# Settling stage of a two-layer kernel: TensorE adds the input, the row factors run one unit behind, rows are stored whole

## What is computed

```python
x = x + attn0(layernorm(x)) + ffn0(layernorm(x))   # ffn0: top 2 of 16 experts by row, plus shared ones
xn = layernorm(x)
x = x + attn1(xn) + ffn1(xn)

def ffn1(input, weight, alpha, bias):              # w_ternary holds only -1, 0 and 1
    return einsum('bsd,od->bso', input, w_ternary * alpha) + bias
# attn1: rows scaled by x / norm(x), times 16 * (gamma + 1), then q, k, v of 16 heads, softmax, output projection
```

## Time and profile before

| | before |
|---|---|
| median of 3 runs | 3088.47 us (3084.22 to 3092.26) |
| the profiled execution, its own time | 3087.61 us |
| its span in the trace | 3085.9 us |
| route and experts, 0 to 598 us | PE busy 494.42 us |
| settle, 598 to 848 us | PE busy 124.87 us, DVE 206.95 us, granted clock 0.62 |
| second layer, from 856 us | PE busy nearly throughout |

### The profile page before, as it was taken

How to read it: one execution, slowest core, us unless ns; L and a number is a source line. 1 busy time by engine, 2 the same in 40 slices (tenths; PEclk the granted TensorE clock), 3 DMA queues, 4 the chain that set the end, 5 groups by cost and what they waited for, 6 DMA issues and landing times.

```text
span 3085.9 us, 46913 instructions
## 1 busy us (share of the span) xinstructions
PE 2810.6 (91%) x13282; PEld 2085.5 (68%) x13282; DVE 2055.1 (67%) x3489; ACT 1839.9 (60%) x2667; POOL 2002.8 (65%) x1246
## 2 busy tenths in 40 slices
PE   6999588655579999999999999999999999999997
PEld 4777456444456777777777777777777777777775
DVE  6887322288866767677676767677676667766763
ACT  4555112122257777777776767777777777777774
POOL 4776400177537777777777777777777777777775
PEclk9999799866689999999999999999999999999998
DMA  4432355588732222222222222231322222232321
GB/s 137 136 123 91 120 172 183 184 257 251 218 87 58 52 73 53 67 60 63 72 48 72 51 69 60 60 78 42 79 46 73 55 64 62 58 77 43 79 47 47
DMA packets 267556, 283.00 MB, mean 92 GB/s; under 512 B 97344, under 2 KB 206144, under 8 KB 267328
## 3 DMA queue, kind: packets, MB, share of 16 engines
q1 hardware_dynamic: 255168, 248.25, 30.0%
q0 software_dynamic: 12288, 33.57, 3.5%
HBM read 131.76 MB, written 82.31 MB: 69 GB/s over the span
## 4 chain that ended last, share of the span: by engine, by line
PE 69%; ACT 1%; DVE 1%; POOL 1%; issue 0%; DMA 0%; SPq 0%; POOLq 0%; ACTq 0%; DVEq 0%
PE psV_b L1527 8%; PE psV_b L1522 7%; PE psV_b L1523 7%; PE psS_b L1510 7%; PE psS_b L1509 7%; PE psN_b L1495 7%; PE psY_b L1450 4%; PE psX_b L1450 4%; PE psY_b L1452 4%; PE psY_b L1451 4%; PE psX_b L1451 4%; PE psX_b L1452 4%; POOL pp_lo_b L1240 1%; PE psN_b L1579 0%; DVE vals_lo_b L1418 0%
## 5 line engine op out<-in xcount | busy, mean ns | idle before, releaser
L1240 POOL TENSOR_TENSOR pp_lo_b<-pf_b,pp_hi_b 128x1024 fp32r<-128x1024 f32 x512 | 1229.8, 2402 | 605.6 <-ACT pp_hi_b L1282 519.8
L1386 DVE TENSOR_REDUCE negmax_b<-psN_b 128x2 fp32r<-128x1024 f32 x512 | 627.1, 1225 | 378.5 <-PE psN_b L1495 370.7
L1277 ACT ACTIVATE pf_b<-psS_b 128x1024 f32<-128x1024 f32 x512 | 526.0, 1027 | 238.9 <-PE psS_b L1510 235.9
L1509 PE MATMUL psS_b<-qA_b,kA_b 128*128 128x512 f32 x1024 | 405.8, 396 | 6.8 <-DVE qB_b L1401 4.9
L1510 PE MATMUL psS_b<-qB_b,kB_b 68*128 68x512 f32 x1024 | 406.6, 397 | 0.0
L1523 PE MATMUL psV_b<-pp_hi_b,vals_lo_b 128*64 128x512 f32 x1024 | 403.5, 394 | 0.0
L1522 PE MATMUL psV_b<-pp_hi_b,vals_hi_b 128*65 128x512 f32 x1024 | 401.8, 392 | 1.4
L1495 PE MATMUL psN_b<-kA_b,qA_b 128*128 128x512 f32 x1024 | 322.5, 396 | 4.6 <-DVE negmax_b L1386 4.1
L1301 ACT ACTIVATE kA_b<-psX_b 64x512 fp32r<-64x512 f32 x256 | 152.0, 594 | 289.7 <-PE psX_b L1452 284.9
L1527 PE MATMUL psV_b<-pp_lo_b,vals_hi_b 128*65 128x512 f32 x1024 | 320.1, 394 | 5.0 <-POOL pp_lo_b L1240 5.0
L1282 ACT ACTIVATE pp_hi_b<-pf_b 128x1024 fp32r<-128x1024 f32 x256 | 271.5, 1061 | 8.1
(11 more groups left out here) (201 smaller groups left out, 5454.4 us busy)
## 6 DMA issues: line engine op xcount, KB each, us to landing
kA_b<-kA_b SPq DMA_DIRECT2D x128, 256.0 KB, 2.9
qB_b<-qA_b SPq DMA_DIRECT2D x128, 256.0 KB, 2.9
inverse_b<-inverse_dram SPq DMA_DIRECT2D x256, 128.0 KB, 3.0
xs_e<-rows_dram SPq DMA_DIRECT2D x144, 128.0 KB, 2.0
results_dram<-ys_e SPq DMA_DIRECT2D x72, 256.0 KB, 2.4
x_a<-x_dram SPq DMA_DIRECT2D x16, 512.0 KB, 4.8
part_dram<-acc_a SPq DMA_DIRECT2D x32, 256.0 KB, 2.1
acc_s<-part_dram SPq DMA_DIRECT2D x32, 256.0 KB
```

Of the source, the lines that this page charges most:

```text
L1240: pool.tensor_tensor(pp[1][:, c], pf[:, c], pp[0][:, c].bitcast(F32), ALU.subtract).then_inc(pl_pool, 1)
L1277: a.activation(pf[:, c], psS[:], ACT.Exp).then_inc(exp_act, 1)
L1386: v.tensor_reduce(negmax[:, n.slot(2), 2 * c:2 * c + 2], psN[:], AX.X, ALU.max, negate=True).then_inc(mx_dve, 1)
L1509: pe.matmul(psS[:, t], kA[:, s, keys], qA[:, s], start=True, stop=False)
```

## The change

Seven edits, the first five in settle:

1. DVE's addition of `x` (L938) goes. PE adds it in `psA`: for each tile an fp32 matmul of `x` with the identity, 256 columns, and then the transposes of `acc` as two ordinary fp32 matmuls that accumulate on it.
2. `xrt` is one fp32 tile, stored whole. DVE's remainder (L921) goes, the ternary weights are fp32, and four fp32 matmuls stand where eight fp32r ones stood.
3. The addition of the last bias (L958) goes from settle; `finish` reads `x1`. In phase_b, DVE adds the bias to `acc` in steps 3 to 6 of the next batch.
4. DVE's loop is `gathered(u)`, `factors(u-1)`, `finish(u-2)`. `f_dve` counts the factors by themselves.
5. `acc` and `x` of the first three units are loaded in the experts' stage (`Ahead`), POOL gathers two units before its loop, and SP loads `gamma` and the first weights behind unit 3.
6. phase_b loads whole rows into two slices of `ot_hi` (`raw_x`) in step 11, and splits them itself: ACT in step 12 (`rows_high`), DVE in steps 12 and 13 (`rows_low`). `otf`'s copies to those slices wait for it.
7. Batch 0 is split at phase_b's start, between the first weights' splits.

```diff
@@ experts, SP @@
+                if n >= PAIRS - 5 and n < PAIRS - 2:
+                    ahead.load(sp, n - PAIRS + 5)
@@ settle, POOL @@
-            for u in range(3):
-                gather(u)
+            gather(0)
+            gather(1)
             for u in range(NU):
-                need(g, s_dve, SD, u, 9)
-                need(g, s_dve, SD, u - 2, SD)
+                need(g, s_dve, SD, u, SD)
+                need(g, f_dve, FC, u - 2, FC)
...
-                gather(u + 3)
+                if u < 2:
+                    gather(u + 2)
+                if u >= 1:
+                    gather(u + 3)
@@ settle, ACT @@
-                need(a, s_dve, SD, u, SD)
+                need(a, f_dve, FC, u, FC)
@@ settle, DVE @@
-                v.tensor_tensor(acc[:, u % 4], psA[:, u % 2].rearrange("p (t d) -> p t d", t=U), x[:, u % 4],
-                                ALU.add).then_inc(s_dve, 1)
...
-                rows_low(u - 1)
-                v.tensor_tensor(x1b[:, u % 3], x1[:, u % 3], fbias_bc[:].unsqueeze(1).to_broadcast([P, U, D]),
-                                ALU.add).then_inc(s_dve, 1)
...
+            for u in range(NU + 2):
+                if u < NU:
+                    gathered(u)
+                if 0 <= u - 1 < NU:
+                    factors(u - 1)
+                finish(u - 2)
@@ settle, PE @@
                     for t in range(U):
+                        pe.matmul(psA[:, u % 2, t * D:(t + 1) * D], kept.ident[:], x[:, u % 4, t], start=True, stop=False,
+                                  skip_group_check=True)
                         for m in range(KD):
                             at = (t * KD + m) * P
-                            mm = pe.transpose(psA[:, u % 2, at:at + P], acc[:, u % 4, m, t * P:(t + 1) * P], kept.ident[:])
+                            mm = pe.matmul(psA[:, u % 2, at:at + P], acc[:, u % 4, m, t * P:(t + 1) * P], kept.ident[:], start=False,
+                                           stop=True, skip_group_check=True)
...
-                need(pe, t_dve, 1, u, 1)
+                need(pe, t_act, 1, u, 1)
...
-                        pe.matmul(out, xrt[0][:, u % 2, t, k], kept.wtern[:, k], start=(k == 0), stop=False)
-                        mm = pe.matmul(out, xrt[1][:, u % 2, t, k], kept.wtern[:, k], start=False, stop=(k == KD - 1))
+                        mm = pe.matmul(out, xrt[:, u % 2, t, k], kept.wtern[:, k], start=(k == 0), stop=(k == KD - 1))
@@ phase_b, SP, ACT, DVE @@
+                if g.const % H == 11 and g.within(0, NH) and batch(g, 1).within(0, B):
+                    after(sp, o_pe, 8, batch(g, -1), 8)
+                    load_x(batch(g, 1))
...
+            def rows_high(b, source):
+                after(a, xt_in, 16, b, 16)
+                a.activation(xT[0][:], source.bitcast(F32), ACT.Copy).then_inc(xh_act, 1)
...
+            def rows_low(b, source, k):
+                after(v, xh_act, 1, b, 1)
+                v.tensor_tensor(xT[1][:, k], source[:, k].bitcast(F32), xT[0][:, k].bitcast(F32), ALU.subtract).then_inc(xl_dve, 1)
...
+                    v.tensor_tensor(acc[:, t], acc[:, t], fbias_bc[:], ALU.add).then_inc(fb_dve, 1)
```

More of the change, by code:

```diff
@@ L96, in __init__, with load @@
         self.ident = sb("ident_f", [P, P])
-        self.wtern = sb("wtern", [P, KD, D], F32R)
+        self.wtern = sb("wtern", [P, KD, D])
         self.alpha_bc = sb("alpha_bc", [P, 1])
         self.table = sb("table", [1, 2 * 2 * P], mybir.dt.uint32)
+class Ahead:
+    def __init__(self, nc, ctx, io, part):
+        self.acc = ctx.enter_context(nc.sbuf_tensor("acc_s", [P, 4, U, D], F32))
+        self.x = ctx.enter_context(nc.sbuf_tensor("x_s", [P, 4, U, D], F32))
+        self.a_in = [ctx.enter_context(nc.semaphore(f"a_in{i}_s")) for i in range(4)]
+        self.part = part
+        self.x_dram = io["x"].rearrange("(u t p) d -> u p t d", t=U, p=P)
+    def load(self, sp, u):
+        sp.dma_start(self.acc[:, u % 4], self.part[u]).then_inc(self.a_in[u % 4], 16)
+        sp.dma_start(self.x[:, u % 4], self.x_dram[u]).then_inc(self.a_in[u % 4], 16)
 def need(eng, sem, per, n, k):
@@ L668, in _, with experts @@
                     pe.matmul(psB[:, 0, 0:1], masks[:, 2], delta[:, 0:1], start=True, stop=True).then_inc(tern_pe, 1)
-def experts(nc, io, rows, results, region, jobs, kept, raw, raw_in):
+def experts(nc, io, rows, results, region, jobs, kept, ahead, raw, raw_in):
     with ExitStack() as ctx:
@@ L785, in _, with settle @@
                 mm.then_inc(y_pe, 1)
-def settle(nc, io, results, part, xT_hi, xT_lo, base_dram, early, kept):
+def settle(nc, io, results, part, xT_dram, base_dram, early, kept, ahead):
     NU = part.shape[0]
@@ L839, in load @@
                 if u < NU:
-                    need(sp, s_dve, SD, u - 4, 5)
-                    sp.dma_start(acc[:, u % 4], part[u]).then_inc(a_in[u % 4], 16)
-                    sp.dma_start(x[:, u % 4], x_dram[u]).then_inc(a_in[u % 4], 16)
-            for u in range(3):
[L845 to L851, removed]
+                    need(sp, s_dve, SD, u - 4, 4)
+                    ahead.load(sp, u)
             for u in range(NU):
@@ L909, in _ @@
                 if u >= 2:
-                    a.wait_ge(stored[u % 2], 80 * (u // 2))
-                a.activation(flat(xrt[0][:, u % 2]), psT[:, u % 2], ACT.Copy).then_inc(t_act, 1)
+                    a.wait_ge(stored[u % 2], 48 * (u // 2))
+                a.activation(flat(xrt[:, u % 2]), psT[:, u % 2], ACT.Copy).then_inc(t_act, 1)
         @block.vector
         def _(v):
[L915 to L922, removed]
             def finish(u):
@@ L943, in _ @@
                     v.scalar_tensor_tensor(out=acc[:, u % 4, t], in0=y[:, u % 4, t, 0], scalar=kept.share[0][:, n:n + 1],
-                                           in1=acc[:, u % 4, t], op0=ALU.mult, op1=ALU.add).then_inc(s_dve, 1)
-                need(v, s_dve, SD, u, 3)
+                                           in1=psA[:, u % 2, t * D:(t + 1) * D], op0=ALU.mult, op1=ALU.add).then_inc(s_dve, 1)
+                need(v, s_dve, SD, u, 2)
                 for t in range(U):
@@ L993, in _ @@
                 need(pe, x_act, U, u, U)
[L994 removed]
+                need(pe, t_act, 1, u - 2, 1)
                 for t in range(U):
@@ L1182, in step @@
                     spread_sums(g)
-                if g.const % H == 12 and g.within(0, NH) and batch(g, 1).within(0, B):
-                    after(sp, kq_pe, 2, pair_at(g, 2), 2)
-                    load_x(batch(g, 1))
                 if p is not None:
@@ L1344, in step @@
                         split_high(c)
-            for c in SPLITS[-4]:
+            split_high(0)
+            rows_high(Step(None, 1, 0), xT[1][:])
+            for c in SPLITS[-4][1:]:
                 split_high(c)
@@ L1390, in step @@
                     maximum(0)
+                t = g.const % H - 3
+                if 0 <= t < TB and batch(g, -1).within(0, B):
+                    b = batch(g, -1)
+                    if b.reg is None and b.const == 0:
+                        v.wait_ge(fb_in, 16)
+                    after(v, o_dve, 8, b, t + 1)
+                    v.tensor_tensor(acc[:, t], acc[:, t], fbias_bc[:], ALU.add).then_inc(fb_dve, 1)
+                if g.const % H == 13 and g.within(0, NH) and batch(g, 1).within(0, B):
+                    rows_low(batch(g, 1), raw_x, 1)
                 if n.within(0, NH):
@@ L1438, in step @@
                         split_low(c)
-            for c in SPLITS[-4]:
+            split_low(0)
+            for k in range(KD):
+                rows_low(Step(None, 1, 0), xT[1][:], k)
+            for c in SPLITS[-4][1:]:
                 split_low(c)
@@ L1603, in two_layers @@
             kept = Kept(nc, first, N // P, jobs)
+            ahead = Ahead(nc, first, io, part)
             with ExitStack() as hold:
@@ L1607, in two_layers @@
                 route(nc, io, rows, part, region, jobs, kept, raw, raw_in)
-                experts(nc, io, rows, results, region, jobs, kept, raw, raw_in)
-            settle(nc, io, results, part, xT_hi, xT_lo, base, early, kept)
-        phase_b(nc, io, xT_hi, xT_lo, base, early)
+                experts(nc, io, rows, results, region, jobs, kept, ahead, raw, raw_in)
+            settle(nc, io, results, part, xT, base, early, kept, ahead)
+        phase_b(nc, io, xT, base, early)
 def lay_out(i):
```

106 lines of the change are left out of this document (52 added, 54 removed).

## The result

The changed kernel takes 3279.17 us (median of 4 runs, 3274.45 to 3283.9) against 3086.82 before: a ratio of 1.0619, 95% interval 1.0606 to 1.0632, 6.2% slower. 3241 was forecast, with a range of 3187 to 3290. The profiled execution has a span of 3275.0 us, 189.1 more than before.

What follows compares the result with a forecast made beforehand. VectorE was taken to bound settle before, a closed lap of 12.47 us a unit after; 3087.6 + 151.6 (settle) + 0.5 (expert-stage loads) + 1.5 (phase_b's start) = 3241 us, range 3187 to 3290.

Steps and rivals of the forecast that it cites:

- The closed lap: Settle: factors(u), `xr`, `psT`, copy, `psF`, `psA`(u+2), gathered(u+2), factors(u+1) form one chain, 12.47 us a unit against 7.19.
- I take `psT` and `psF` low and `psA` high: Choice of TensorE's clock level in each unit of settle; gives 3.40 us for `psF` and 2.14 for `psA`.
- factors: In settle's unit, from VectorE's factors to the start of ScalarE's `xr`: 1.12 us.
- copy: In settle's unit, the copy behind `psT` with its hand-over: 0.66 us.
- gathered: In settle's unit, VectorE from L943 to the end of the variances: 2.85 us.
- The two starts of the earlier trace: TensorE after waits: after 5.48 us idle, high 3.46 us later; after 2.71 us idle, low throughout 4.7 us.
- Hidden edits: Edits outside settle's chain: expert-stage loads 0.5 us, phase_b's start 1.5 us; later splits and 64 bias additions nothing.
- The clock stays low in `psA` too: Rival in settle: `psA` also at the low clock, 48 us more, 3289 us; chance 0.13.
- the likeliest case: Settle at 12.47 us a unit, 3241 us in all, own range 3220 to 3265; chance 0.62.
- The clock rises inside `psF`: Rival in settle: 11.6 us a unit, 26 us less, 3215 us; chance of an earlier clock 0.20.
- No change: Rival: settle's chain is loose in part of the units and costs what VectorE gains, 3088 us; chance 0.02.
- Faster: Rival: GpSimd's 6.28 us a unit binds settle, 28 us less, 3058 us; chance 0.03.

Runs made afterwards that it cites:

- Both ways of opening it: Changed kernel with one edit each: TensorE issues `psA`(u+2) ahead of `psT`/`psF`(u), 3066.46 us; or VectorE's factors(u) back in gathered(u)'s turn, 3069.72 us.
- three copies: Changed kernel plus three VectorE copies of 512 fp32 elements a row into an unread tile, between its wait for `psA` and L939: 3281.01 us.
- loads ahead: Changed kernel with TensorE's `psA` of unit u+2 ahead of `psT`/`psF` of u, and SP's loads of `acc` and `x` one unit further ahead: 3058.17 us.
- the order alone opened: Changed kernel with one edit: TensorE issues `psA` of unit u+2 ahead of `psT` and `psF` of unit u; 3066.46 us, ratio 0.994.

## Why the prediction was right, and where a size was off

**The closed lap was right.** It was read from the two orders and the waits, and the trace shows it: VectorE waits 30 times for `psA` (9 us each, where 7 were forecast), TensorE 31 times for `xr`, 5.2 us as forecast. Both ways of opening it bring 210 us.

**Mis-sized: the clock in `psA`.** The step that failed is "I take `psT` and `psF` low and `psA` high", of which the second half held in full only in the first lap. The terms measured in the lap shown above, in the order of the forecast: factors 1.11 (1.12), `xr` 1.14 (1.15), `psT` 1.15 (1.15), copy 0.65 (0.66), `psF` 3.57 (3.40), `psA` 3.26 (2.14), gathered 2.78 (2.85). The sum is 13.66 against 12.47, and 1.12 of the 1.19 is `psA`. The two starts of the earlier trace rows suggested a rise some 3.5 us after `psF` begins. In the first lap it came even a little earlier, in the end of `psF`, all of `psA` ran high, and the lap took 624.07 - 611.81 = 12.26 us, near the 12.47 forecast:

```profile
618.71 3.47 PE L1007 MATMUL psF_s<-wtern,xrt_s 128*128 128x256 f32 x8 [0.69 <-ACT xrt_s L918]
622.02 0.59 PE L984 MATMUL psA_s<-x_s,ident_f 128*128 128x256 f32 x2
624.07 0.87 DVE L939 SCALAR_TENSOR_TENSOR acc_s<-y_s,share,psA_s 128x256 f32<-128x256 f32 x2 [8.34 <-PE psA_s L988]
```

But the forecast took one start after a wait for all of them, and the rise moves from lap to lap. It came 4.4 us behind `psF`'s start in the second lap and 5.3 in the third; the laps grew over 12.94, 13.19, 13.48 and 13.55 us to 13.66. In the lap shown above it came at about 812.9, 6 us after `psF` began and 8 after `psT`. With three copies the laps come down to the same length from above: 14.39, 14.03, 13.85, 13.75. So the lap is held at 13.66 us, and the rise falls where that leaves it. What sets this length no run here shows.

**Where the 189.1 us of span went.** Factors(0) started at 614.65, forecast 613.85: 0.8. Factors(30) started at 1021.25; (1021.25 - 614.65) / 30 = 13.55 us, so 30 laps took 406.6 - 374.1 = 32.5 us more than forecast. From there to the last `finish` at 1034.45 it took 13.20 us where 11.18 was forecast, mostly because `psF`(31) ran at the low level. Together 35.3, which is 186.9 (1034.45 less the 847.56 of the earlier trace rows) less the 151.6 forecast. The last 2.2 us are the second layer.

**Hidden edits, right.** The second layer's first matmul in TensorE's timeline of the kernel before:

```profile
855.92 0.76 PE L1450 MATMUL psX_b<-xT_hi,wqkv_hi_b 128*128 128x512 f32 x1 [8.40 <-DVE wqkv_lo_b L1361]
```

The last `finish` to this matmul took 855.92 - 847.56 = 8.36 us before and 9.64 after: 1.3 more, forecast 1.5. From that matmul to the end, 2230.9 us against 2230.0: the later batches' splits, the 64 bias additions and the load in step 11 cost nothing measurable. VectorE's wait for `y` ended at 606.78 where it had ended at 610.04.

**The rivals.** "The clock stays low in `psA` too" (3289) was nearest, with 0.13; the likeliest case, 3241 with a range of its own of 3220 to 3265, missed. "The clock rises inside `psF`" (3215) is seen only in the last part of the first lap's `psF`. "No change" fell with the 192 us. "Faster" fell with the order closed, but its numbers hold once it is open: GpSimd's 6.28 us a unit was forecast, and 6.27 was measured. That its 3058 is the time of loads ahead, 3058.17, is in part luck: with the order alone opened it is 3066.46, and loads ahead has one edit more.

## What to carry to other kernels

When work is moved a step behind on one engine, write down for each engine what now stands in front of it, and follow the waits until they come back to the start. If the circle closes after one unit, its pieces add up, and no engine's busy time tells it. Then move an item that nobody in the circle needs yet (here six matmuls) in front of the wait; and read the next bound from the engine that has the longest round by itself.

## What had not been expected of the hardware

A chain that alternates idle time and matmuls can be held at a fixed length by TensorE's clock: laps of 13.66 us with 0, 0.34 and 1.01 us added to the chain, approached from below and from above, and no hold with 1.68 us added or with a shorter `psA` (12.34 and 11.56 us). Within the hold, what is added to the chain reads as nothing, so a piece of it can't be priced by adding to it.

With a gap of 2.57 us before `psT` and one of 0.69 us behind it, the clock went from the high level in `psT` to the low one in `psF`; with gaps of 0.42 and 0.25 us and `psT` and a filler matmul between them it stayed at 1.00. Matmuls whose results nobody reads made the closed lap 3.4 us shorter.
